# One third of the down product as three float32r passes

## What is computed

```python
y = conv_depthwise_7x7(x, dw_w) + dw_b
y = layernorm_over_channels(y) * ln_w + ln_b
y = einsum('bhwc,cd->bhwd', y, w1) + b1          # 96 -> 384, "up"
y = gelu(y)
gx = sqrt(sum(y**2, axis=(1, 2)))                # one number per image and hidden channel
nx = gx / (mean(gx, axis=-1) + 1e-6)
y = grn_gamma * (y * nx) + grn_beta + y          # GRN
y = einsum('bhwd,dc->bhwc', y, w2) + b2          # 384 -> 96, "down"
x = x + y
xq = clip(floor(x * 65536) / 65536, -32768, 32767)
out = conv_depthwise_3x3(xq, w rounded to powers of 2) + bq
```

## Time and profile before

| | before |
|---|---|
| median of 3 runs | 1080.56 us (1080.2 to 1081.1) |
| profiled execution | 1080.37 us |
| its span, first to last instruction | 1078.6 us |
| mean granted TensorE clock | 0.963 |
| busy: TensorE, VectorE, ScalarE, GpSimd | 92%, 77%, 77%, 38% |
| first depthwise stage | about 0 to 365 us |
| middle stage (16 images) | about 385 to 877 us |
| second depthwise stage | about 885 to 1078 us |

### The profile page before, as it was taken

How to read it: one execution, slowest core, us unless ns; L and a number is a source line. 1 busy time by engine, 2 the same in 40 slices (tenths; PEclk the granted TensorE clock), 3 DMA queues, 4 the chain that set the end, 5 groups by cost and what they waited for, 6 DMA issues and landing times.

```text
span 1078.6 us, 21092 instructions
## 1 busy us (share of the span) xinstructions
PE 990.8 (92%) x5574; PEld 717.7 (67%) x5574; DVE 825.5 (77%) x1768; ACT 830.8 (77%) x1724; POOL 411.7 (38%) x353
## 2 busy tenths in 40 slices
PE   3999999999999467999999999999999849999996
PEld 2788888888888355666666666666666427767774
DVE  7777777777777565888888888888887667888885
ACT  2688888888887357898988888888888607787874
POOL 2666676666666153332333333333332001111110
PEclk9999999999999766999999999999999978999999
DMA  8777777777772592555555555555543247999995
GB/s 162 147 183 182 181 179 184 187 187 179 180 179 66 131 225 82 157 175 163 172 162 171 172 162 170 162 171 162 167 136 90 80 110 187 245 248 243 247 244 154
DMA packets 146312, 182.95 MB, mean 170 GB/s; under 512 B 13799, under 2 KB 140424, under 8 KB 143208
## 3 DMA queue, kind: packets, MB, share of 16 engines
q1 hardware_dynamic: 145480, 179.97, 62.5%
q10 hardware_dynamic: 800, 2.61, 1.0%
HBM read 124.28 MB, written 58.25 MB: 169 GB/s over the span
## 4 chain that ended last, share of the span: by engine, by line
PE 71%; DVE 12%; ACT 6%; issue 6%; DMA 3%; DVEq 1%; POOL 0%; ACTq 0%; SPq 0%; POOLq 0%
PE psum L573 22%; PE psum L653 21%; PE psum L643 6%; PE psum L644 6%; PE psum L645 6%; PE psum L552 6%; PE psum L600 3%; DVE arena_r L894 3%; ACT arena L706 2%; ACT arena_r L691 2%; DVE arena L919 1%; DMA arena<-lines_a 1%; DVE arena L923 1%; DVE arena L1079 1%; DVE arena L1068 1%
## 5 line engine op out<-in xcount | busy, mean ns | idle before, releaser
L573 PE MATMUL psum<-arena_r 112*128 112x464 f32 x1536 | 375.2, 386 | 0.3 <-issue 0.2
L573 PEld LDWEIGHTS psum<-arena_r 112*128 112x128 f32 x1536 | 276.8, 190 | 33.9 <-issue 1.1
L653 PE MATMUL psum<-arena,w2s 128*96 128x448 f32 x672 | 266.8, 542 | 2.8 <-DVE w2s L994 2.8
L787 ACT ACTIVATE arena<-psum,b1g 128x448 f32<-128x448 f32 x336 | 201.8, 630 | 58.3 <-PE psum L645 58.2
L497 POOL TENSOR_TENSOR arena_r<-arena,arena_r 96x448 fp32r<-96x448 f32 x112 | 134.1, 1197 | 268.7 <-DVE arena_r L969 194.8
L653 PEld LDWEIGHTS psum<-arena,w2s 128*96 128x96 f32 x672 | 109.8, 164 | 119.1 <-issue 111.8
L643 PE MATMUL psum<-arena_r,w1h 96*128 96x448 f32 x336 | 154.1, 459 | 14.2 <-POOL arena_r L497 13.0
L706 ACT ACTIVATE arena<-psum,bias_a 64x224 f32<-64x224 f32 (+1 forms) x288 | 117.0, 442 | 61.8 <-PE psum L573 50.6
L894 DVE TENSOR_TENSOR arena_r<-psum,arena_r 112x224 fp32r<-112x224 f32 x384 | 127.2, 382 | 48.3 <-ACT arena_r L691 47.5
L691 ACT ACTIVATE arena_r<-psum 112x224 fp32r<-112x224 f32 x384 | 112.6, 355 | 54.8 <-PE psum L552 52.5
L486 POOL TENSOR_TENSOR arena<-arena 128x448 f32<-128x448 f32 x96 | 110.0, 1146 | 109.8 <-DVE arena L923 109.2
(11 more groups left out here) (94 smaller groups left out, 1146.1 us busy)
## 6 DMA issues: line engine op xcount, KB each, us to landing
arena<-lines_a SPq DMA_DIRECT2D x48, 448.0 KB
arena<-in_x_dram SPq DMA_DIRECT2D x48, 392.0 KB
y_scratch<-arena SPq DMA_DIRECT2D x48, 392.0 KB
arena<-in_x_dram SPq DMA_DIRECT2D x112, 168.0 KB, 2.5
z_scratch<-arena SPq DMA_DIRECT2D x112, 168.0 KB, 2.0
arena<-z_scratch SPq DMA_DIRECT2D x48, 392.0 KB
out_dram<-arena SPq DMA_DIRECT2D x48, 392.0 KB
arena_r<-y_scratch SPq DMA_DIRECT2D x98, 168.0 KB, 2.6
```

The source lines that it names most:

```text
L573: mm = nc.tensor.matmul(p_conv[s % 2][:, 0:NCOL], w[:, p, s, TW * k:TW * k + TW], v[:, p, s, slot0 + k:slot0 + k + JP, :].rearrange("p j i ...
L653: mm = nc.tensor.matmul(p_o[k][0:C, 0:CH], w2s[:, p, m, :], hid[:, p, m, CH * t:CH * t + CH], start=(m == 0), stop=(m == MT - 1))
L787: nc.scalar.activation(hid[:, p, m, CH * t:CH * t + CH], p_h[m][:, 0:CH], ACT.Gelu, bias=b1g[:, m:m + 1]).then_inc(gelu_done, 1)
```

## The change

For m = 0, one of the three groups of 128 rows, the float32 product is replaced by three float32r passes as in `up`: w2h*gh, w2h*gl, w2l*gh. The products of m = 1 and 2 stay float32, and come first; then TensorE waits for the low part (gl_ready). VectorE makes the high part gh of hid[m=0] (`hid_high`, a cast of 128x448) at the start of each chunk, at t = 6 behind grn_sums; GpSimd makes the low part gl (`hid_low`, a subtraction of 128x448) ahead of `low` of the same t, at t = 6 behind gx. Both have two buffers. grn_scale gets two more operations of 96 columns, w2h and w2l, in its chain. The arena shrinks by the room that the new tiles take.

```diff
@@ -117,6 +117,10 @@
         b1g = sb("b1g", [128, MT])
         w2r = sb("w2r", [128, MT, C])
         w2s = sb("w2s", [128, 2, MT, C])
+        w2h = sb("w2h", [128, 2, C], F32R)
+        w2l = sb("w2l", [128, 2, C], F32R)
+        gh = sb("gh", [128, 2, CH], F32R)
+        gl = sb("gl", [128, 2, CH], F32R)
         gam = sb("gam", [128, MT])
         bet = sb("bet", [128, MT])
         lnw = sb("lnw", [C, 1])
@@ -134,7 +138,7 @@
 
 
 
-        ARENA, ARENA_R = 28672, 18816
+        ARENA, ARENA_R = 26432, 18816
         arena = sb("arena", [128, ARENA])
         arena_r = sb("arena_r", [128, ARENA_R], F32R)
 
@@ -254,6 +258,8 @@
         gsum_done = sem("gsum_done")
         grn_step = sem("grn_step")
         w2_ready = sem("w2_ready")
+        gh_ready = sem("gh_ready")
+        gl_ready = sem("gl_ready")
         o_done = sem("o_done")
         v_ready = sem("v_ready")
         r_ready = sem("r_ready")
@@ -497,6 +503,12 @@
                 pool.tensor_tensor(yl[:, CH * t:CH * t + CH], ct[:, (t + p) % 2, :], yh[:, CH * t:CH * t + CH].bitcast(F32),
                                    ALU.subtract).then_inc(yn_ready, 1)
 
+            def hid_low(i, p, t):
+
+                k = (t + p) % 2
+                pool.wait_ge(gh_ready, NCH * i + t + 1)
+                pool.tensor_tensor(gl[:, k, :], hid[:, p, 0, CH * t:CH * t + CH], gh[:, k, :].bitcast(F32), ALU.subtract).then_inc(gl_ready, 1)
+
             def step(i, p):
                 fixed = isinstance(i, int)
                 for t in range(NCH):
@@ -504,6 +516,8 @@
 
                         pool.wait_ge(ss_ready, i + 1)
                         pool.tensor_tensor(gx[:, :], ss3[:, :], halves[:, :], ALU.pow).then_inc(gx_ready, 1)
+                    if not (fixed and i == 0):
+                        hid_low(i - 1, 1 - p, t)
                     if not (fixed and i >= NIMG - 1):
                         low(i + 1, 1 - p, t)
 
@@ -649,9 +663,12 @@
                     pe.wait_ge(w2_ready, i + 1)
                 need(pe, v_ready, NCH * i + t - 1)
                 k = (t + p) % 2
-                for m in range(MT):
-                    mm = nc.tensor.matmul(p_o[k][0:C, 0:CH], w2s[:, p, m, :], hid[:, p, m, CH * t:CH * t + CH],
-                                          start=(m == 0), stop=(m == MT - 1))
+                for m in range(1, MT):
+                    nc.tensor.matmul(p_o[k][0:C, 0:CH], w2s[:, p, m, :], hid[:, p, m, CH * t:CH * t + CH], start=(m == 1), stop=False)
+                pe.wait_ge(gl_ready, NCH * i + t + 1)
+                nc.tensor.matmul(p_o[k][0:C, 0:CH], w2h[:, p, :], gh[:, k, :], start=False, stop=False)
+                nc.tensor.matmul(p_o[k][0:C, 0:CH], w2h[:, p, :], gl[:, k, :], start=False, stop=False)
+                mm = nc.tensor.matmul(p_o[k][0:C, 0:CH], w2l[:, p, :], gh[:, k, :], start=False, stop=True)
                 mm.then_inc(o_done, 1)
 
             def step(i, p):
@@ -978,7 +995,7 @@
 
             def grn_scale(i, p):
 
-                n = 5 * i
+                n = 7 * i
                 dve.wait_ge(gsum_done, i + 1)
                 dve.tensor_reduce(gsum[:, :], p_grn[p], AX.X, ALU.add).then_inc(grn_step, 1)
                 dve.wait_ge(grn_step, n + 1)
@@ -990,9 +1007,19 @@
                 dve.wait_ge(grn_step, n + 4)
                 dve.tensor_scalar(gsc[:, :], gnx[:, :], FIX, FIX, ALU.mult, ALU.add).then_inc(grn_step, 1)
                 dve.wait_ge(grn_step, n + 5)
-                for m in range(MT):
-                    ins = dve.tensor_scalar(w2s[:, p, m, :], w2r[:, m, :], gsc[:, m:m + 1], None, ALU.mult)
-                ins.then_inc(w2_ready, 1)
+                dve.tensor_scalar(w2s[:, p, 0, :], w2r[:, 0, :], gsc[:, 0:1], None, ALU.mult).then_inc(grn_step, 1)
+                for m in range(1, MT):
+                    dve.tensor_scalar(w2s[:, p, m, :], w2r[:, m, :], gsc[:, m:m + 1], None, ALU.mult)
+                dve.wait_ge(grn_step, n + 6)
+                dve.tensor_copy(w2h[:, p, :], w2s[:, p, 0, :]).then_inc(grn_step, 1)
+                dve.wait_ge(grn_step, n + 7)
+                dve.tensor_tensor(w2l[:, p, :], w2s[:, p, 0, :], w2h[:, p, :].bitcast(F32), ALU.subtract).then_inc(w2_ready, 1)
+
+            def hid_high(i, p, t):
+
+                dve.wait_ge(gelu_done, MT * (NCH * i + t) + 1)
+                need(dve, o_done, NCH * i + t - 1)
+                dve.tensor_copy(gh[:, (t + p) % 2, :], hid[:, p, 0, CH * t:CH * t + CH]).then_inc(gh_ready, 1)
 
             def residual(i, p, t):
 
@@ -1043,6 +1070,7 @@
                         grn_sums(i, p)
 
 
+                    hid_high(i - 1, 1 - p, t)
                     for norm, rnd in ((scale, residual), (high, nearest), (None, above), (None, floor_of)):
                         if norm and ahead:
                             norm(i + 1, 1 - p, t)
```

## The result

The changed kernel takes 1156.7 us (1155.4 to 1161.4, four runs) against 1080.6 us before: a ratio of 1.0712 with a 95% interval of 1.0681 to 1.0742. Forecast were 1180 us, with a range of 1135 to 1206. The profiled execution took 1155.4 us, its span is 1153.6. One of the experiments, the one with chunk 6 left in float32, took 1119 to 1122 us in three executions and 1150 us in two; its number is of the three.

A forecast was written before the change was run, and what follows sets the result against it. The prediction took TensorE to bound the kernel (71% of the chain), with VectorE little behind. To 1080.4 us it added 72 (68 for the hold, 4 for the last step) and 28 for the clock: 1180 us, range 1135 to 1206.

The forecast's parts named there:

- The hold of down(6) and down(0): Middle stage: TensorE waits there for low parts, +4.65 us per image (+3.1 the first), 68 us in all.
- Who is late at chunk 6: End of an image: hid_high(6), behind grn_sums, waits for ScalarE's squares, done at 30.0 to 30.3 us into the step.
- U+28.8: Time within an image's step; U is its start on TensorE, the end of the previous down(6).
- VectorE's load as a rival: Middle stage: only VectorE's own work counts, 30.5 us per image, +1.6 each, 1103 us; chance 0.07.
- TensorE's gain: In down: three float32r passes replace one float32 product, saving 0.143 us per chunk, 1.0 per image, 16 us.
- grn_scale's two operations: VectorE's grn_scale: a rounding and a subtraction of 96 columns add 0.43 us to 1.57, bounds 0.2 and 0.8.
- The clock: Middle stage: standstills bring the lower clock in nearly each image, +1.9 us per image (0 to 3.5), 28 over 15.
- the first rival I named: The clock doesn't fall, or seldom, as short work splits the standstill: 1152 us, 1166 if half the time; clock up 0.14.
- The last step: Last step of the middle stage: VectorE alone sets the pace, and gx to first down gets longer; +4 us.
- The signs: Trace marks: images 35 to 36 us, idle in down(6) and down(0) released by GpSimd, mean clock about 0.9.

The follow-up runs named there:

- VectorE's and GpSimd's added work without any hold (1129.2): Changed kernel with hid_high and hid_low made in every chunk, but down stays three float32 products and waits for none of them: 1129.2 us, 1.0452.
- the waits and passes but the clock up (1144.9): Changed kernel plus needless float32r passes on TensorE, 6 ahead of the wait in down(5) and 9 ahead of that in down(6): 1144.9 us, 1.0596.
- The run with the casts together: Changed kernel with VectorE's chunk reordered to scale, hid_high, high, then residual, nearest, above, floor_of: 1173.7 us, 1.0878.
- the kernel without the subtractions: Kernel before plus VectorE's hid_high casts and grn_scale's two operations, without GpSimd's hid_low; down keeps three float32 products: 1085.9 us, 1.0050.

## Why the prediction was right, and where it wasn't

The sign and the place were right: 76 us slower of the 100 forecast, all in the middle stage. The sum came out partly by luck. The forecast had 72 us for the hold with the last step, and 28 for the clock. The runs have 49 us for VectorE's and GpSimd's added work without any hold (1129.2), 16 more with the waits and passes but the clock up (1144.9), and 12 for the clock. So two thirds of the cost come from what I had only as a rival, priced at 23 us and given a chance of 0.07. Step by step:

- **The hold of down(6) and down(0).** The waits are there as forecast, their price isn't. All 72.7 us of standstill ahead of the first new pass are released by hid_low. Per image it was 1.3 to 1.4 us in down(0) (1.6 forecast), and 1.4 to 1.7 in down(5) and 1.9 to 2.0 in down(6). I had put the last two on down(6) alone, as 4 us. hid_low(6) lands 2.25 us after grn_sums (648.75 + 1.12 - 647.62), not 2.85: from gx to the next operation it was 0.90 and not 1.46. And the wait isn't the price of the hold: with VectorE's list at 32.5 us per image by itself, the hold adds only some 0.8 us to an image (33.4 on average at full clock), where I had 4.65 on 28.95.
- **Who is late at chunk 6.** Half right, by luck. I forecast that hid_high(6), due at U+28.8, waits for the squares at 30.0. In the trace VectorE comes to grn_sums 0.25 to 0.75 us after the squares, but for the first three images and the last. The term that failed is chunk 1: I took 3.95 us from one hid_high to the next, and it is 5.59 (660.99 to 666.58), since low(0) and hid_low(1) run back to back and `scale` waits out both. The pattern of one subtraction between two casts held in the other chunks (3.93 to 4.03 measured, 3.95 forecast). The two ends came out within a microsecond of each other, so the period was hardly touched: 33.1 and 33.65 us at full clock, forecast as 33.6. The run with the casts together shows that the squares would have held it otherwise.
- **VectorE's load as a rival.** Its 30.5 us were 32.5, by the same chunk 1 and five chunks of 4.0. At 1129 instead of 1103 us it is the largest single cost. The failed term is the exclusion: I let one subtraction hold one cast by 0.4 us, and the kernel without the subtractions is 43 us faster.
- **TensorE's gain.** The passes do save 16 us of TensorE, but with them alone the kernel gains 8. Chunks of 3.93 to 3.94 us are there, in the last ones too, so ScalarE's 4.07 doesn't slow them; 4 of the 8 us are TensorE's wait for gx behind the squares.
- **grn_scale's two operations.** 2.00 us from the first to residual (654.32 to 656.32), as forecast.
- **The clock.** 1.5 us per fall (35.18 - 33.65) against 1.9. Wrong in how often: behind the first image it fell in 6 of 14, not in nearly all, and cost 12 us instead of 28. The standstill came in two pieces with passes between, which is the first rival I named (1166 with half the falls). This is 16 of the 23 us by which the forecast was too high. Of the other 7, some 2.6 are the images' 33.4 instead of 33.6, and 2.3 the last one, which grew by 2.4 us (28.55 to 30.94) and not by 4.65.
- **The last step.** +3.8 us against +4.
- **The signs.** Down(0) waits 1.3 us and is released by hid_low, as named. The image period is 33.1 and 35.2 us and not 35 to 36, and the mean clock 0.954 and not 0.9.

## What to carry to other kernels

Before work is moved to an engine with idle time, ask which operations of its neighbour it shuts out: 7 GpSimd subtractions per image cost 43 us in all, though GpSimd had been idle for two thirds of the middle stage (9.5 of 28.9 us busy). Operations that exclude each other go together in one block, and those that read PSUM beside the other engine's. And where a new operand is made in a queue, put it ahead of that queue's waits (sums, roots) which depend on later work of the consumer. One of the two isn't enough: grouping alone made the kernel slower (1174 us), moving the operand alone brought 0.3 us per image at full clock. Together, with the first two casts behind the weights' chain, the same operations took 1076 us instead of 1157. And where a run hits the expected time, look at its granted clock before the reason is believed.

## What the runs showed of the hardware

- A VectorE operation that is shut out by GpSimd doesn't get in between two GpSimd operations that stand back to back: `scale` issued at 661.29 waited for both, 661.24 to 663.50, and took 2.69 us. Even operations on three columns, 0.17 us otherwise, took 1.06 beside GpSimd's subtractions (663.77 to 666.09). The Trainium skill ("SBUF — State Buffer", Who interferes with whom) says that a VectorE operation with two SBUF inputs contends with GpSimd, and of VectorE's 2-port mode that whoever issues first gets the shared pair for the whole instruction. The trace agrees (`scale`, two SBUF inputs, 0.61 us when nothing is beside it), and adds the case of two in a row.
- The granted clock can go either way behind nearly the same gaps. Behind gaps of 1.55 and 2.01 us at 645.57 and 649.93, with passes between, it was down (650.50 to 653.90 at 0.50, 1.2 GHz); in the image before, behind gaps of 1.38 and 1.91 us, it stayed up (616.90 to 620.30 at 1.00, 2.4 GHz).

```profile
612.06 0.45 PE L669 MATMUL psum<-gh,w2h 128*96 128x448 f32 x1 [1.38 <-POOL gl L510]
616.33 0.45 PE L669 MATMUL psum<-gh,w2h 128*96 128x448 f32 x1 [1.91 <-POOL gl L510]
```

```profile
616.90:620.30 3.40, 3.40 (x20) 3.18 (x19) 2.38 (x9) 2.99 (x6) 0.94 (x1) 1.00 0.45 127
```
